# Splitting the attention weights in the keys' loop instead of the expert loop, and storing the result by tiles

## The reference, cut to what matters

```python
x = x + L0_xattn(ctx, layernorm(x), ...)      # a state space model: convolution, scan, gate
x = x + L0_ffn(layernorm(x), ...)             # 64 experts, top 8 per token
x = x + L1_xattn(layernorm(x), ctx, Wq, Wk, Wv, Wo, gq, gk)
x = x + L1_ffn(layernorm(x), w1, w2)          # 512 -> 2048 -> 512, gelu, ternary weights

def L1_xattn(h, e, Wq, Wk, Wv, Wo, gq, gk):   # 16 heads of 128
    q = rmsnorm(heads(h @ Wq), gq)
    k = rmsnorm(heads(e @ Wk), gk)            # depends on ctx alone
    v = heads(e @ Wv)                         # depends on ctx alone
    return merge(softmax(q @ k.T / sqrt(128)) @ v) @ Wo
```

## Time and profile before

| | |
|---|---|
| median of 3 runs | 2832.93 us (2829.97 to 2833.83) |
| profiled execution: time, span | 2839.08 us, 2837.6 us |
| mean granted TensorE clock | 0.948 of 2.4 GHz |
| busy share of the span | PE 88%, weight load 62%, DVE 66%, ACT 45%, POOL 54% |
| DMA | 572.10 MB, mean 202 GB/s |

### The profile page before, as it was taken

One profiled execution on the slowest core, in us unless ns is written; L12 is line 12 of the kernel. 1 busy time (PEld: TensorE's weight loads), 2 busy tenths in 40 slices (PEclk: granted clock), 3 DMA queues, 4 the chain that ended last, 5 costly groups with the idle time before them and its releaser, 6 DMA issues. The chain is left out here.

```text
span 2837.6 us, 42365 instructions
## 1 busy us (share of the span) xinstructions
PE 2485.7 (88%) x11365; PEld 1766.0 (62%) x11366; DVE 1863.6 (66%) x3083; ACT 1280.9 (45%) x2516; POOL 1542.7 (54%) x1262
## 2 busy tenths in 40 slices
PE   6898987679793899999999937999999999999797
PEld 2333432267572677777777725778778777877553
DVE  6999999868462346654444456776775776565596
ACT  4566664343562333321222204555555555555385
POOL 2656565432555667676666545655664764444122
PEclk8999999979896899999999967999999999999899
DMA  6989898735675999987777654543444443332101
GB/s 201 289 271 296 267 295 270 218 138 197 237 271 198 334 339 315 342 287 257 265 264 247 204 170 141 180 140 125 158 138 135 159 156 112 123 115 90 60 1 60
DMA packets 271500, 572.10 MB, mean 202 GB/s; under 512 B 26993, under 2 KB 92657, under 8 KB 270593
## 3 DMA queue, kind: packets, MB, share of 16 engines
q1 hardware_dynamic: 218080, 381.54, 40.8%
q0 software_dynamic: 44032, 167.80, 17.6%
q10 hardware_dynamic: 9248, 21.11, 2.2%
HBM read 361.69 MB, written 208.67 MB: 201 GB/s over the span
## 5 line engine op out<-in xcount | busy, mean ns | idle before, releaser
L625 POOL TENSOR_TENSOR b_u<-du,bc 128x1024 f32<-128x1024 f32 x128 | 301.0, 2352 | 214.6 <-DVE c_state L699 111.7
L451 PE MATMUL ps_y<-c_state,ident 128*128 128x512 f32 x512 | 253.6, 622 | 89.0 <-DVE c_state L699 89.0
L2004 ACT ACTIVATE prob<-ps_s,neg,q_rs 128x512 f32<-128x512 f32 x256 | 197.0, 774 | 265.0 <-DVE neg L2194 265.0
L690 DVE TENSOR_TENSOR_SCAN state<-ps_decay,b_u 128x1024 f32<-128x1024 f32 x128 | 292.7, 2287 | 14.6 <-POOL b_u L625 2.3
L1521 PE MATMUL ps_o<-w_dn,hid_t 96*128 x632 | 297.5, 593 | 0.0
L1557 ACT ACTIVATE silu_g<-ps_gu 128x192 f32<-128x192 f32 x159 | 52.5, 330 | 530.1 <-PE ps_gu L1502 530.1
L2098 POOL TENSOR_SCALAR prob<-prob,rden 128x512 f32<-128x512 f32 x256 | 174.7, 692 | 199.9 <-DVE rden L2202 199.9
L451 PEld LDWEIGHTS ps_y<-c_state,ident 128*128 128x128 f32 x512 | 92.9, 194 | 233.6 <-DVE c_state L699 143.8
L1502 PE MATMUL ps_gu<-w_gu_high,rows_t_high 128*128 (+1 forms) x636 | 228.4, 359 | 9.7 <-POOL w_gu_low L1387 8.0
L1387 POOL TENSOR_TENSOR w_gu_low<-raw_gu,w_gu_high 128x1536 fp32r<-128x1536 f32 x64 | 223.8, 3497 | 11.7 <-POOL w_gu_high L1385 11.7
L523 ACT ACTIVATE ps_decay<-delta,a_neg 128x511 f32<-128x511 f32 x256 | 165.6, 681 | 142.2 <-DVE state L690 141.2
(11 more groups left out here) (349 smaller groups left out, 6051.8 us busy)
## 6 DMA issues: line engine op xcount, KB each, us to landing
bc<-bc_dram SPq DMA_DIRECT2D x128, 512.0 KB
raw_gu<-in_gate_up POOLq DMA_DIRECT2D x64, 768.0 KB, 6.0
rows<-rows_dram SPq DMA_DIRECT2D x160, 256.0 KB, 4.8
y_dram<-y SPq DMA_DIRECT2D x158, 256.0 KB, 4.4
rows_dram<-zeros SPq DMA_DIRECT2D x46, 768.0 KB
w_q<-wq_dram SPq DMA_DIRECT2D x64, 512.0 KB, 3.7
w_o<-wo_dram SPq DMA_DIRECT2D x16, 2048.0 KB, 9.6
w_dn<-in_down POOLq DMA_DIRECT2D x64, 384.0 KB, 6.4
```

The source lines that it names most:

```text
L451: mm = pe.matmul(ps_y[e][:, :], c.ident[:, :], c_state[:, q % 2, g, :], start=False, stop=False)
L625: pool.tensor_tensor(out=b_u[:, q % 2, :, :], in0=slot(du, n).rearrange("p (a l) -> p a l", a=1).broadcast_to([P, G, SEQ]), in1=bc[:, g % ...
L690: dve.tensor_tensor_scan(state[:, q % 2, :], decay[q % 2][:, :], b_u[:, q % 2, :, :].rearrange("p g l -> p (g l)"), 0.0, ALU.mult, ALU.add ...
L2004: act.activation(prob[:, qt, :], ps_s[qt % 2][:, :], ACT.Exp, scale=q_rs[:, k % 2, qt:qt + 1], bias=neg[:, qt:qt + 1], accum_out=den[:, qt ...
```

## The change

The split of W_q and W_o leaves `experts` and goes into the keys' loop of `dispatch`. There are 16 pairs of heads, one for each of the 16 groups of four tiles: in head group `hg` the groups r = 0 and 1 split a pair of W_q each, r = 2 and 3 a pair of W_o each. The high part is now an ACT instruction, the low part a DVE instruction, and SP issues the loads and stores. The raw and split buffers have two slots, r % 2. `rolled` gets a third argument, which on ACT runs `heads_high` at the start of the steps g = 1 to 4, ahead of the squares. On DVE `heads_low` stands at the end of each group. Besides, `store_output` is gone: SP stores each tile of the result in `feed_forward` as soon as it is added.

```diff
-        def rolled(eng, first, second):
+        def rolled(eng, first, second, also=None):
             with eng.Fori(0, ST) as hg:
                 for g in range(NG4 + 1):
+                    if also and g >= 1:
+                        also(hg, g - 1)
                     if g < NG4:
                         for s, n in steps(hg, g):
                             first(hg, s, n)
...
+            def load_heads(hg, r):
+                sp.wait_ge(aw_low, pair_no(hg, r) + 1)
+                for h in range(2):
+                    head, to = hg * ST + r % 2 * 2 + h, raw_w[:, r % 2, h, :]
+                    if r < 2:
+                        ins = sp.dma_start(to.rearrange("p (k n) -> p k n", k=KD),
+                                           d["w_q"][bass.ds(head, 1), :, :].rearrange("a p (k n) -> (a p) k n", k=KD))
+                    else:
+                        ins = sp.dma_start(to, d["w_o"][bass.ds(head * HD, HD), :])
+                    ins.then_inc(aw_loaded[r % 2], 16)
+
+            def store_heads(hg, r):
+                sp.wait_ge(aw_low, pair_no(hg, r) + 3)
+                for h in range(2):
+                    head = bass.ds(hg * ST + r % 2 * 2 + h, 1)
+                    to = (m.wq_dram[head, ...] if r < 2 else m.wo_dram[head, ...])
+                    sp.dma_start(to, words(out_w[:, r % 2, h, :, :]...)).then_inc(aw_stored[r % 2], 16)
+
             with sp.Fori(0, ST) as hg:
                 for n in range(NT):
+                    if n % G4 == 0:
+                        load_heads(hg, n // G4)
+                    if n in (8, 12):
+                        store_heads(hg, (n - 8) // G4)
                     sp.wait_ge(k_kept, hg * NT + n + 1 + KB)
                     sp.dma_start(m.k_dram[...], k_out[:, n % G4, :]).then_inc(k_stored[n % G4], 16)
+                store_heads(hg, 2)
+                store_heads(hg, 3)
...
+            def heads_high(hg, r):
+                act.wait_ge(aw_loaded[r % 2], hg * 64 + r // 2 * 32 + 32)
+                act.wait_ge(aw_stored[r % 2], hg * 64 + r // 2 * 32 + 32)
+                act.activation(out_w[:, r % 2, :, 0, :], raw_w[:, r % 2, :, :], ACT.Copy).then_inc(aw_high, 1)
...
+            rolled(act, square, keep, heads_high)
...
+            def heads_low(hg, r):
+                dve.wait_ge(aw_high, pair_no(hg, r) + 1)
+                dve.tensor_tensor(out=out_w[:, r % 2, :, 1, :], in0=raw_w[:, r % 2, :, :], in1=out_w[:, r % 2, :, 0, :],
+                                  op=ALU.subtract).then_inc(aw_low, 1)
...   (experts: load_heads and split_heads are taken out, and the loop over the slots runs 1 to 14 in one piece)
-            load_heads("w_q", 0)
             for slot in range(WS):
                 load_raw(slot, slot)
...   (feed_forward)
+        @block.sync
+        def _(sp):
+            for t in range(NT):
+                sp.wait_ge(y_added, t + 1)
+                sp.dma_start(out[t * P:(t + 1) * P, :], c.X[:, t, :]).then_inc(stored, 16)
+            sp.wait_ge(stored, 16 * NT)
...
-def store_output(nc, c, out):
```

More of the change, by code:

```diff
@@ L1153, in dispatch, with pair_no @@
         ROOT_STEPS = 12
+        raw_w = p.sb("raw_aw", [P, 2, 2, DM])
+        out_w = p.sb("out_aw", [P, 2, 2, 2, DM], F32R)
+        aw_loaded = [p.sem("aw_loaded0"), p.sem("aw_loaded1")]
+        aw_stored = [p.sem("aw_stored0"), p.sem("aw_stored1")]
+        aw_high, aw_low = p.sem("aw_high"), p.sem("aw_low")
+        def pair_no(hg, r):
+            return hg * ST + r
         def steps(hg, g):
             return [(hg * NT + g * G4 + t, g * G4 + t) for t in range(G4)]
-        def rolled(eng, first, second):
+        def rolled(eng, first, second, also=None):
             with eng.Fori(0, ST) as hg:
                 for g in range(NG4 + 1):
+                    if also and g >= 1:
+                        also(hg, g - 1)
                     if g < NG4:
@@ L1176, in _ @@
                 sp.sem_inc(k_stored[i], 16)
+            for i in range(2):
+                sp.sem_inc(aw_stored[i], 32)
+            def load_heads(hg, r):
[12 more added lines that the diff above has]
+                    head = bass.ds(hg * ST + r % 2 * 2 + h, 1)
+                    to = (m.wq_dram[head, :, :, :, :].rearrange("a p x k n -> (a p) (x k n)") if r < 2 else
+                          m.wo_dram[head, :, :, :].rearrange("a p x n -> (a p) (x n)"))
+                    sp.dma_start(to, words(out_w[:, r % 2, h, :, :].rearrange("p x n -> p (x n)")))\
+                        .then_inc(aw_stored[r % 2], 16)
             with sp.Fori(0, ST) as hg:
                 for n in range(NT):
+                    if n % G4 == 0:
+                        load_heads(hg, n // G4)
+                    if n in (8, 12):
+                        store_heads(hg, (n - 8) // G4)
                     sp.wait_ge(k_kept, hg * NT + n + 1 + KB)
@@ L1181, in _ @@
                                  k_out[:, n % G4, :]).then_inc(k_stored[n % G4], 16)
+                store_heads(hg, 2)
+                store_heads(hg, 3)
             for i in range(G4):
                 sp.wait_ge(k_stored[i], 16 * KVS // G4 + 16)
+            for i in range(2):
+                sp.wait_ge(aw_stored[i], 32 * ST * 2 + 32)
         @block.gpsimd
@@ L1243, in _ @@
             act.wait_ge(gain_made, 1)
-            rolled(act, square, keep)
+            rolled(act, square, keep, heads_high)
         @block.vector
@@ L1298, in _ @@
                                           op=ALU.mult).then_inc(k_normed, 1)
+                    heads_low(hg, g)
 def experts(nc, c, m, d):
@@ L1428, in _ @@
                 expert(0, slot, first=True)
-            split_heads("w_q", 0, 0, ("w_q", 1))
-            with pool.Fori(1, J - 1) as e4:
+            with pool.Fori(1, NE // WS - 1) as e4:
                 for slot in range(WS):
                     expert(e4, slot)
-                split_heads("w_q", e4, e4, ("w_q", e4 + 1))
             for slot in range(WS):
[L1435 to L1444, removed]
+                expert(NE // WS - 1, slot, last=True)
         @block.sync
@@ L2356, in _, with feed_forward @@
                 add(NPP - 1, 1, t, last_banks[t])
-def feed_forward(nc, c, m):
+def feed_forward(nc, c, m, out):
     with ExitStack() as ctx:
@@ L2385, in feed_forward @@
         h_half_clipped, hq_half_made = p.sem("h_half_clipped"), p.sem("hq_half_made")
+        stored = p.sem("stored")
+        @block.sync
[4 more added lines that the diff above has]
+            sp.wait_ge(stored, 16 * NT)
         def schedule(eng, *parts):
@@ L2627, in program @@
             norm_statistics(nc, c, "n3", loads, first=(BATCH - 1) * ST)
-            feed_forward(nc, c, m)
-        store_output(nc, c, out)
-def store_output(nc, c, out):
[L2633 to L2638, removed]
+            feed_forward(nc, c, m, out)
 def kernel(x, ctx_1024, L0_xattn_in_proj_w, L0_xattn_conv_w, L0_xattn_conv_b, L0_xattn_x_proj_w,
```

4 lines of the change are left out of this document (1 added, 3 removed).

## The result

The changed kernel takes 2884.96 us (median of 4 runs, 2878.63 to 2890.05) where the kernel before takes 2833.38 us: ratio 1.0176, interval 1.0144 to 1.0209. It is slower by 51.6 us; the forecast was 2902 us, 17 us too much, with a range of 2860 to 2928.

The account below looks back on a forecast made before the run. PE bounds the experts and POOL's sends the end of dispatch, where ACT's load waits would take over. Profiled 2839.1 + 78.0 + 5 - 4 - 10.2 = 2907.9 us, +68.8; on the 2832.9 median about 2902 us, range 2860 to 2928.

Parts of the forecast that it names:

- What bounds: PE bounds the experts, so removing POOL's split buys nothing there; shrinking PE's idle time gives -2 us (0 to -3.6).
- The end: After the last add: waiting for a 0.26 MB tile's store instead of 4.19 MB saves 10.2 us (9 to 11.5).
- the first load: Start of experts: the heads' load ahead of the first expert's load goes, -1.2 to -2.6 us, taken as -2.
- Compute: 0 to 2 us a head group beside the waits: Keys' loop: added ACT and DVE work is mostly hidden, costing 0 to 2 us a head group, within 30 us spare.
- There is no lead: Keys' loop: SP issues each load behind ACT's last keep, so ACT stalls; 38.4 us of stalls a slow-pace head group.
- the quick pace: Keys' loop after the sends: SP's queue has the engines alone, stalls total 20.8 us, a head group takes 50.8 us.
- The sends end by 915: Dispatch: POOL's 102 sends come every 1.76 us beside SP's added bytes, ending at 915 us.
- The second rival: Dispatch: loads in time but DMA full, 68.7 MB take 183 us, ending at 920, +9; time 2828 us; chance 4%.
- The end of dispatch, +78.0: Dispatch: stalled head groups and last stores move its end from 910.9 to 988.9 us; SP's queue ends last, not POOL's.
- PE's clock, 5 us: Keys' loop: idling in stalls drops PE to 1.2 GHz, costing 0 to 19 us; 5 taken.
- the savings: Experts and program end: -4 us in the experts and -10.2 us from the last store.
- The rule for two busy rings: Dispatch upper case: engines alternate between busy rings, SP's queue gets half of 376 GB/s, dispatch ends at 998, +87.

Follow-up runs that it names:

- experiment 5: Kernel before plus 16 high-part activations on ACT and 16 low-part subtractions on DVE on scratch buffers, no other traffic: 2837.72 us, ratio 1.0013.
- experiment 2: Changed kernel with every load of a pair of heads issued one group of tiles earlier, stores left in place: 2868.70 us, ratio 1.0129.
- experiment 3: Changed kernel with every pair's store issued one group of tiles earlier, loads left in place: 2866.58 us, ratio 1.0128.
- experiment 4: Changed kernel with both loads and stores of the heads issued one group earlier: 2864.32 us, ratio 1.0111.
- experiment 7: Changed kernel with the heads' loads and stores one group earlier and four sends in flight instead of two: 2819.06 us, ratio 0.9952.
- experiment 9: Changed kernel with four sends in flight instead of two, nothing else changed: 2967.61 us, ratio 1.0477.
- experiment 10: Kernel before with stores by tiles, four sends in flight, and POOL's first load of heads behind the four experts' loads: 2911.28 us, ratio 1.0272.
- experiment 8: Kernel before with stores by tiles and four sends in flight instead of two, the split left in the experts: 2774.09 us, ratio 0.9799.
- experiment 1: Kernel before with only the result's stores by tiles, as in the change: 2822.54 us, ratio 0.9965.
- experiment 6: Kernel before plus the heads' loads and stores on SP at the change's places, ACT and DVE not using them: 2885.03 us, ratio 1.0189.
- experiment 11: The kernel of experiment 8, unchanged, run again on a third chip: 2772.87 us, ratio 0.9777.
- experiment 12: The kernel of experiment 10, unchanged, run again on a third chip: 2767.43 us, ratio 0.9783.

## Why the prediction was right, and where it was off

*What bounds.* Right. PE bounds the experts, and the 25 us of POOL's time that left 272 us there bought 2.1 us in the whole of experts and attention (-2 was taken). This pair of runs can't tell 2.1 us: over all 14 traces the stretch takes 1733 to 1738 us in the eight of kernels that split in the experts and 1728 to 1735 in the six of kernels that don't, 5 us less in the mean. The end gave -10.9 (-10.2 predicted), the first load -1.9 (-2).

*Compute: 0 to 2 us a head group beside the waits.* Nearly: with nothing else added the keys' strand grew by 10 us for four head groups where 0 to 8 were allowed, and the time by nothing that could be told (experiment 5).

*There is no lead.* Right, and it sets the time of after. From the first square to the last keep 240.3 us were predicted and 238.9 measured. The head groups came at 58.3, 68.4, 62.8 and 50.8 us by the forecast; they took 56.4, 60.8, 63.8 and 57.9. Two errors offset each other; that it came out within 1.4 us is luck. ACT's own work was put at 120 us in all and is 106, about 25.6 in each of the last three head groups: PE had run ahead during the stalls, and the squares of a group took 2.9 us instead of 3.5 and, right behind a head group's last keeps, 3.0 instead of 5.6. The stalls were put at 120 us and are 132.9: those of the last head group sum to 32.3 us instead of the 20.8 of the quick pace, because the sends lasted until 943.

*The sends end by 915.* Wrong: they ended at 943, and this is the one failure in kind. The step took SP's bytes as spread over the stage and gave a send 1.76 us; it was 2.16. The earlier trace rows shows full DMA in the loop already in the kernel before, with share 0.72 on average: with 25 MB more, two sends in flight get what SP's queue leaves. In after this is hidden by 23 us, as 942.15 + 0.97 + 11.2 is 954.3 and the block ended at 977.6. It is why none of the three other orders of SP's stream that were tried saved the change (experiments 2 to 4). The second rival, "the loads are in time, but DMA is full", has its premise in experiment 4 and failed by 36 us there: 2864 instead of 2828. It counted bytes at full rate, which two sends in flight didn't draw: 181 to 205 GB/s once SP's queue is empty. Its 183 us are nearly reached with four (196.4, experiment 7).

*The end of dispatch, +78.0.* Sign and place right, 8.4 us too long. From the last keep I counted 7.9 us for the last stores and 9.2 for the change of blocks, which is the distance in the earlier trace rows from landing to next block; it was 8.7 in all. The 9.2 us were POOL's drain of 8.39 us after its last send, not a cost of the seam: where POOL is done early it lies beside the keys.

*PE's clock, 5 us.* Right that it falls (0.79 in the loop, products at 7.95 us), wrong that it shows: PE waits for ACT, and the slow products end before ACT needs them; from 735 to 970 us ACT waits for PE twice, 1.0 us in all. So 78.0 + 5 = 83 stand against 68.2: 8.4 for the seam, 5 for the clock and 1.4 for the strand make the 14.8. With the savings that is +68.8 against +53.2; the other 2 us between the forecast and the result are run-to-run.

*The rule for two busy rings.* The Trainium skill ("DMA: Bandwidth & Descriptors", Queues, rings and completion order) has each DMA engine take the busy rings in turn, from which half each was worked out, +87. In experiment 4, where POOL kept two sends in flight, SP's queue got 76% and the sends 22%: even more than the 225 of 376 GB/s that I took from the rows. With four sends in flight it was 66% and 37% (experiment 7), so the sends' share went up with their number in flight. Whether POOL's ring always had work, which the rule asks for, no trace shows; half each is what neither depth gave, and the measurement decides.

**What is open.** Why, on one chip, the other engines made only one step in 10 us beside POOL's unbroken sends (experiments 9 and 10), while the kernel of 10 ran well on a second and that of 8 on a second and a third. All runs of 9 and 10 were made on that chip at one time, so a lasting trait of the chip and a passing state of it can't be told apart. On the good chips, too, POOL waited for DMA ahead of 8 of the 102 sends only and sent one every 1.31 us (experiment 8; 1.29 in 10), so the sends' pace alone is not it, nor were the DMA engines full (0.55 from 780 to 870 us in 10). In the routing stage already PE was slow on that chip (busy 20 and 22 us of 35 from 677 to 712, against 28 to 34 in the other kernels with four in flight). It was not tried what four in flight do to the changed kernel as it is on another chip, nor three in flight; so what ACT's waits would cost by themselves, with the sends out of the way, is not measured.

**The best version.** Stores by tiles, four sends in flight, the split left in the experts, with or without the edit of experiment 10: 2767 to 2774 us on two chips, 2.0 to 2.2% faster than before, but 2911 on a third (only timed there with that edit). The version that keeps clear of this is that of experiment 1, 2822.5 us, with two sends in flight; it was timed on one chip.

## What to carry to other kernels

A load that is issued behind the output of its own consumer has no lead: read in the issuing queue what stands ahead of it, and price the wait, not the instruction. Before work is moved into a stage for its idle engines, count the bytes that move with it and ask which queue they displace, and whether that queue has enough in flight to win the time back afterwards; here two limits, 251 and 238 us, lay one behind the other, and mending the first showed the second. Whatever is finished early should be stored early: 16 small stores beside the last stage cost nothing and saved 11 us.

## What the runs showed of the hardware

- The dispatch block, in which POOL issues 102 indirect DMAs, ends with a drain of 8.39 us on POOL, the same in all 14 traces; the routing block, in which it issues 26, ends with one of 4.1 us with two sends in flight and 6.2 to 7.1 us with four. From the end of the last send's issue to the next block's first issue 11.2 us pass where POOL is last and has two in flight, and 12.8 with four (experiment 7).
- With two indirect DMAs in flight (256 KB each, 128 rows of 2 KB) beside a busy SP queue, that queue holds 76% of the engines and a send comes every 2.8 to 3.0 us (experiments 4 and 6); with four in flight the sends' share of the engines rises from 22% to 37% (experiment 7). Alone, two in flight draw about 180 to 205 GB/s, half of what the engines moved in the same runs.
- With four in flight and only the keys' stores beside them, POOL issues one every 1.3 us, nearly without a wait (experiments 8, 11 and 12); beside the heads' traffic it is one every 1.8 us, with 76 waits (experiment 7).
- One and the same kernel took 2767 us on one chip and 2911 on another, each steadily, while the kernel before took 2832 on that other one: a gain seen on one chip alone may not hold on the next.
